# Cross attention with scores over row halves of the tensor engine, and a written-out round for every engine

## What is computed

```python
x = _layernorm(x + _L0_attn_ref(x, ...))                 # causal self-attention, 16 heads of 8
x = _layernorm(x + _L0_xattn_ref(ctx_1024, x, mask, ...))
x = _layernorm(x + _L0_ffn_ref(x, ...))                  # 8 experts, top 2, and a shared one

def _L0_xattn_ref(x, latents, mask, g1, b1, g2, b2, Wq, Wkv, Wout):
    heads, dim_head = (16, 64)
    xn = layer_norm(x, g1, b1)                           # 512 context rows
    ln_lat = layer_norm(latents, g2, b2)                 # 256 tokens
    q = ln_lat @ Wq
    kv = jnp.concatenate([xn, ln_lat], axis=1) @ Wkv     # 768 keys
    ...
    weight = jnp.einsum('bhld,bhnd->bhln', q * scale, k * scale)
    weight = jax.nn.softmax(jnp.where(full_mask, weight, neg), axis=-1)
    out = jnp.einsum('bhln,bhnd->bhld', weight, v)
    return out @ Wout
```

## Time and profile before

| | us |
|---|---|
| median of 3 runs | 1220.61 |
| lowest, highest | 1219.43, 1220.95 |
| span of the profiled execution | 1221.5 |
| PE busy in it | 1123.2 (92%) |
| DVE busy | 879.1 (72%) |
| ACT busy | 755.0 (62%) |
| POOL busy | 418.3 (34%) |

### The profile page before, as it was taken

One profiled execution on the slowest core, in us unless ns is written; L12 is line 12 of the kernel. 1 busy time (PEld: TensorE's weight loads), 2 busy tenths in 40 slices (PEclk: granted clock), 3 DMA queues, 4 the chain that ended last, 5 costly groups with the idle time before them and its releaser, 6 DMA issues. The chain is left out here.

```text
span 1221.5 us, 29151 instructions
## 1 busy us (share of the span) xinstructions
PE 1123.2 (92%) x8775; PEld 967.0 (79%) x8775; DVE 879.1 (72%) x2777; ACT 755.0 (62%) x1779; POOL 418.3 (34%) x453
## 2 busy tenths in 40 slices
PE   2998898399999999989999989999999986899996
PEld 2877777278888888878888878888888866899996
DVE  3998897687777787867787857787876755555555
ACT  2998997377666766756776756776766754222222
POOL 4554453134433434433433432533433424000000
PEclk9999999699999999999999999999999996899998
DMA  5000021000000000000000000000000000000001
GB/s 172 7 6 5 5 87 40 1 1 1 1 2 1 2 2 2 1 4 2 2 2 1 2 4 2 1 1 1 2 2 1 2 1 1 1 1 0 0 1 35
DMA packets 11403, 12.31 MB, mean 10 GB/s; under 512 B 1152, under 2 KB 9344, under 8 KB 11136
## 3 DMA queue, kind: packets, MB, share of 16 engines
q1 hardware_dynamic: 8032, 5.90, 1.7%
q10 hardware_dynamic: 3232, 4.73, 1.2%
HBM read 9.57 MB, written 1.05 MB: 9 GB/s over the span
## 5 line engine op out<-in xcount | busy, mean ns | idle before, releaser
L803 POOL TENSOR_TENSOR xk_parts<-k_raw,xk_parts 64x768 fp32r<-64x768 f32 x128 | 236.5, 1848 | 444.2 <-DVE xk_parts L895 444.2
L919 DVE CUSTOM_DVE_ANT_0 xmasked<-ps,bar 128x768 f32<-128x768 f32 x256 | 244.2, 954 | 6.0 <-issue 1.6
L852 ACT ACTIVATE xprobs<-xmasked,xlow 128x768 f32<-128x768 f32 x256 | 238.1, 930 | 6.1 <-issue 5.3
L999 PE MATMUL ps<-xk_parts,xq_parts 128*128 128x512 f32 (+1 forms) x1024 | 232.9, 349 | 4.5 <-DVE xq_parts L900 2.7
L1005 PE MATMUL ps<-ident,xprobs 128*128 128x128 f32 x1536 | 215.0, 276 | 1.5 <-DVE xprobs_t L924 1.1
L999 PEld LDWEIGHTS ps<-xk_parts,xq_parts 128*128 128x128 f32 x1024 | 175.1, 190 | 28.9 <-DVE xq_parts L900 3.2
L1016 PE MATMUL ps<-xprobs_t,xvals 128*64 128x256 f32 x1536 | 179.9, 383 | 1.1 <-ACT xprobs_t L858 1.1
L1005 PEld LDWEIGHTS ps<-ident,xprobs 128*128 128x128 f32 x1536 | 169.3, 140 | 9.4 <-DVE xprobs_t L924 1.3
L1016 PEld LDWEIGHTS ps<-xprobs_t,xvals 128*64 128x64 f32 x1536 | 104.7, 137 | 57.9 <-issue 10.5
L924 DVE COPY xprobs_t<-ps 128x768 f32<-128x768 f32 x128 | 121.6, 950 | 4.5 <-PE ps L1005 4.5
L112 DVE MEMSET xspare<- 128x1 f32 x256 | 15.1, 59 | 148.5 <-PE ps L999 114.6
(11 more groups left out here) (183 smaller groups left out, 2395.4 us busy)
## 6 DMA issues: line engine op xcount, KB each, us to landing
w_up<-in_L_ffn_w SPq DMA_DIRECT2D x2, 1024.0 KB, 6.8
raw_kv<-in_L_xattn_Wkv ACTq DMA_DIRECT2D x1, 1024.0 KB, 5.3
x_in<-in_x SPq DMA_DIRECT2D x8, 128.0 KB, 2.2
out<-state SPq DMA_DIRECT2D x4, 256.0 KB, 2.6
raw_q<-in_L_xattn_Wq ACTq DMA_DIRECT2D x1, 512.0 KB, 6.6
keep_all<-in_mask_BxS_bk ACTq DMA_DIRECT2D x1, 512.0 KB, 14.0
wout<-in_L_xattn_Wout ACTq DMA_DIRECT2D x1, 512.0 KB, 6.7
w_up<-in_L_ffn_sw SPq DMA_DIRECT2D x2, 128.0 KB, 4.0
```

Of the source, the lines that this page charges most:

```text
L803: pool.tensor_tensor(k_parts[dst, i // 2 % 2, h, :], k_raw[src, :], k_parts[src, i // 2 % 2, h, :].bitcast(F32), ALU.subtract).then_inc(k_ ...
L852: nc.scalar.activation(probs[:, i % 4, :], masked[:, i % 4, :], ACT.Exp, scale=-1.0, bias=low[:, i % 4:i % 4 + 1], accum_out=sums[:, pair ...
L919: dve.tensor_tensor_reduce(masked[:, i % 4, :], slot(slots.place("S", i), KEYS), bar[:, par, :], 1.0, 3e38, ALU.add, ALU.min, low[:, i % 4 ...
L999: last = nc.tensor.matmul(slot(s, hi - lo, lo), q_parts[:, pair % 2, h, part, t * P:(t + 1) * P], k_parts[:, pair % 2, h, lo:hi], start=pa ...
```

## The change

The split parts are no longer stacked. `q_parts[:, i % 2, 0]` is the rounded q of both heads of a pair, `[..., 1]` its rest, each with head 0 on rows 0 to 63 and head 1 on rows 64 to 127; `k_parts` likewise. S1 makes the scores of both heads for one half of the queries: three products (high by high, high by rest, rest by high) of 64 rows each per head, head 0 and head 1 in turn, into two slots, which S0 and S1 take. Rest by rest is left out. TWICE is gone; HI, Q and LO are one instruction of 128 partitions per pair.

PSUM: three wide slots remain. Q, R, TX and OUT share one narrow bank (`NARROW_BANK`); PV has one bank (`HEADS_BANK`) in place of two. The order is written out: a round per pair for each engine, with the once-a-batch steps at fixed rounds.

```diff
-    pe_order = Order(B, UNITS, {
-        "S": (UNITS, -2.25), "K": (PAIRS, -5.75), "Q": (PAIRS, -7.25), "V": (PAIRS, -4),
...
+    def pe_round(p):
+        yield from (("S0", 2 * p), ("S1", 2 * p), ("PT", 4 * p - 2), ("Q", p + 1), ("K", p + 1), ("PT", 4 * p - 1),
+                    ("V", p + 1))
+        if p == 4:
+            yield "TC", 1
+        yield from (("S0", 2 * p + 1), ("S1", 2 * p + 1), ("PT", 4 * p), ("PV", p - 1), ("PT", 4 * p + 1), ("R", p - 1))
+        if p == 1:
+            yield "OUT", -1
+        if p == 3:
+            yield "TX", 1
+
+    def dve_round(p):
+        if p == 2:
+            yield from (("OUT", -1), ("NORMED", 1), ("BAR", 1))
+        if p == 5:
+            yield "Y", 1
+        yield from (("S", 4 * p), ("S", 4 * p + 1), ("PT", 2 * p - 1), ("RECIP", p - 1), ("NORM", p - 2),
+                    ("Q", p + 1), ("HI", p + 1))
+        yield from (("S", 4 * p + 2), ("S", 4 * p + 3), ("PT", 2 * p))
+
+    def act_round(p):
+        yield "R", p - 2
+        if p == 4:
+            yield "TX", 1
+        yield from (("PT", 2 * p - 1), ("Q", p + 1), ("EXP", 4 * p), ("K", p + 1), ("EXP", 4 * p + 1), ("V", p + 1))
+        if p == 4:
+            yield "TC", 1
+        yield from (("PT", 2 * p), ("EXP", 4 * p + 2), ("EXP", 4 * p + 3))
+
+    def pool_round(p):
+        if p == 5:
+            yield "Y", 1
+        yield from (("WIDE", p - 1), ("LO", p + 1))
...
+    NARROW = ("Q", "R", "TX", "OUT")
+    wide = Turns(pe_order, [k for k in full if k not in NARROW], SLOTS)
+    narrow = Turns(pe_order, NARROW, 1)
+    NARROW_BANK, HEADS_BANK = O_BANK, O_BANK + 1
...
+                if kind == "S1":
+                    pair, t = i // 2, i % 2
+                    pe.wait_ge(k_ready, b * PAIRS + pair + 1)
+                    pe.wait_ge(q_ready, b * PAIRS + pair + 1)
+                    places = wide.place("S0", i), s
                     for lo, hi in ((0, C), (C, KEYS)):
-                        for part in range(2):
-                            last = nc.tensor.matmul(slot(s, hi - lo, lo), q_parts[:, pair % 2, h, part, t * P:(t + 1) * P],
-                                                    k_parts[:, pair % 2, h, lo:hi], start=part == 0, stop=part == 1)
-                    last.then_inc(full["S"], 1)
+                        for n, (qp, kp) in enumerate(((0, 0), (0, 1), (1, 0))):
+                            for h in range(2):
+                                rows = slice(h * XD, (h + 1) * XD)
+                                last = nc.tensor.matmul(slot(places[h], hi - lo, lo),
+                                                        q_parts[rows, pair % 2, qp, t * P:(t + 1) * P],
+                                                        k_parts[rows, pair % 2, kp, lo:hi], start=n == 0, stop=n == 2)
+                    last.then_inc(full["S1"], 1)
...
-                    wait(pe, heads_ready, n - 1)
+                    wait(pe, heads_ready, n)
```

More of the change, by code:

```diff
@@ L21 @@
 from contextlib import ExitStack
+from functools import partial
 import concourse.bass as bass
@@ L79, in run, with __init__ @@
         one(self.batches, self.batches)
+class Sequence(Order):
+    def __init__(self, batches, rounds, counts, pattern):
+        self.batches = batches
+        self.steps = []
+        for p in range(rounds):
+            for kind, n in pattern(p):
+                rel, i = divmod(n, counts[kind])
+                self.steps.append((kind, rel, i))
+        for kind, count in counts.items():
+            assert sorted(i for k, _, i in self.steps if k == kind) == list(range(count)), kind
+        assert all(-1 <= rel <= 1 for _, rel, _ in self.steps)
 class Turns:
@@ L735, in cross_attention @@
     normed_ready = sem("x_normed_ready")
-    full = {k: sem(f"x_{k}_full") for k in ("TC", "TX", "K", "Q", "V", "S", "PT", "R", "OUT")}
+    full = {k: sem(f"x_{k}_full") for k in ("TC", "TX", "K", "Q", "V", "S0", "S1", "PT", "R", "OUT")}
     yc_ready, yx_ready = sem("x_yc_ready"), sem("x_yx_ready")
@@ L740, in cross_attention @@
     kh_done, k_ready = sem("x_kh_done"), sem("x_k_ready")
[L741 to L742 removed]
+    qh_done, q_ready = sem("x_qh_done"), sem("x_q_ready")
     v_ready = sem("x_v_ready")
@@ new lines, in pool_round @@
+    def pool_round(p):
+        if p == 5:
+            yield "Y", 1
+        yield from (("WIDE", p - 1), ("LO", p + 1))
+    once = {"OUT": 1, "TC": 1, "TX": 1}
+    pairs = {"K": PAIRS, "Q": PAIRS, "V": PAIRS, "R": PAIRS}
+    pe_order = Sequence(B, PAIRS, {**once, **pairs, "S0": XH, "S1": XH, "PT": UNITS, "PV": PAIRS}, pe_round)
+    dve_order = Sequence(B, PAIRS, {"S": UNITS, "PT": XH, "Q": PAIRS, "HI": PAIRS, "RECIP": PAIRS, "NORM": PAIRS,
+                                    "OUT": 1, "NORMED": 1, "BAR": 1, "Y": 1}, dve_round)
@@ L830, in emit @@
                     act.wait_ge(full["K"], b * PAIRS + i + 1)
-                    wait(act, k_ready, b * XH + 2 * i)
-                    nc.scalar.activation(k_raw[:, :], slot(slots.place("K", i), KEYS), ACT.Copy).then_inc(k_out, 1)
+                    wait(act, k_ready, b * PAIRS + i)
+                    nc.scalar.activation(k_raw[:, :], slot(wide.place("K", i), KEYS), ACT.Copy).then_inc(k_out, 1)
                 if kind == "Q":
                     act.wait_ge(full["Q"], b * PAIRS + i + 1)
[L835 to L839, removed]
+                    wait(act, full["S1"], b * XH + 2 * (i - 1))
+                    nc.scalar.activation(q_parts[:, i % 2, 0, :], narrow_bank(S),
+                                         ACT.Copy, scale=Q_SCALE).then_inc(qh_done, 1)
                 if kind == "V":
@@ L956, in emit @@
                 if kind in full:
-                    s = slots.place(kind, i)
-                    earlier = slots.before(kind, b, i)
+                    turns = narrow if kind in NARROW else wide
+                    s = turns.place(kind, i)
+                    earlier = turns.before(kind, b, i)
                     if earlier:
@@ L963, in emit @@
                     for n, j in enumerate(range(CT) if kind == "TC" else range(CT, KT)):
-                        last = nc.tensor.transpose(slot(s, P, n * P), normed[:, j, :], ident[:, :])
+                        last = nc.tensor.transpose((narrow_bank if kind == "TX" else partial(slot, s))(P, n * P), normed[:, j, :], ident[:, :])
                     last.then_inc(full[kind], 1)
```

102 lines of the change are left out of this document (38 added, 64 removed).

## The result

| | us |
|---|---|
| before, median | 1220.12 |
| after, median of 4 | 1265.11 (1263.31 to 1266.53) |
| after / before | 1.0366, 95% interval 1.0351 to 1.0381 |

The change makes the kernel 45 us slower. The forecast had it 20 slower: the sign is right, the size less than half. 1265 is above the range of the likeliest case (1224 to 1257), and inside only the wide one, 1208 to 1281. The profiled execution of after took 1263.31 us.

The account below looks back on a forecast made before the run. The prediction took the order and length of tensor work as the bound: -8.5 us from ordinary rounds and +28.2 from batch turns gave +19.7, so 1240 us. The likeliest case ranged from 1224 to 1257, 8 in 10 from 1208 to 1281.

Parts of the forecast that it names:

- Part 3: Ordinary round with the ring of three wide PSUM places: 11.09 us against 11.22, 8.5 us gained over 64 rounds.
- the walk: Step-by-step timing of one tensor-engine round, S1 first at 0, from group lengths and waits: 11.09 us.
- Part 4: Turn of a batch: added waits cost 4.03 us each, +28.2 us for seven turns.
- part (b): Batch turn: OUT, stats, NORMED and BAR in one vector-engine piece before the first mask make K wait 2.16 us more.
- part (a): Batch turn: OUT and TX each wait for the scalar engine to copy R from the shared bank, 0.64 us each.
- Part (c): Batch turn: with TC behind V, the second S1 waits for V's place, 0.49 us.
- part (d): Batch turn: Y ahead of a mask, 0.2 us.
- Part 1: Scores: row halves run in pairs, an S1 takes 1.30 us with its shape changes, 0.24 us gained a pair.
- halves in turn: Rival on the scores: row halves don't overlap, each S1 1.05 us longer, 134 us more, 1374 us; chance 9%.
- serial weight loads: Rival on the scores: products pair up but their weight loads don't, 38 us more, 1278 us; chance 12%.
- free change of shape: Rival on the scores: entering a row-halved shape costs nothing, 32 us less, 1208 us; chance 19%.
- Part 2: Vector engine and gpsimd lose cast, HI, Q and LO work that was off the path: worth nothing directly.

Follow-up runs that it names:

- full rows: S1 as two 128-row products per head in place of three 64-row ones: 1278.14 us in the changed kernel, 1227.62 us with the order moves and swap added.
- all moves: Changed kernel with R and OUT behind the first S1, K before Q in OUT's round, TC, NORMED and BAR moved, the mask's waits swapped: 1223.63 us.
- the first experiment: Changed kernel with S1 as two products over all 128 rows per head, in the new order and layout: 1278.14 us, ratio 1.0471 to the kernel before.

## Why the prediction was wrong in size

**Part 3, the ordinary round: this step failed.** It forecast 11.09 us, 0.13 less than before; measured 11.43, 0.21 more. Over the stage that is -8.5 (0.13 x 64 is 8.3) against +13.2, 22 of the 25 us that the forecast is short of. Some rows of the kernel before, from the pair of the earlier trace rows, that the walk did not use:

```profile
490.49 0.94 PE L999 MATMUL ps<-xk_parts,xq_parts 128*128 128x512 f32 x4
491.26 0.84 PE L1005 MATMUL ps<-ident,xprobs 128*128 128x128 f32 x6
491.96 0.39 PE L989 MATMUL ps<-wv_hi,y_hi 128*128 128x256 f32 x1
...
493.12 0.86 PE L999 MATMUL ps<-xk_parts,xq_parts 128*128 128x512 f32 x4
493.82 0.28 PE L978 MATMUL ps<-y_hi,wq_hi 128*128 128x256 f32 x1
```

The round by its groups, each from its start to the start of the next, any wait behind it included:

| us | before | walk | after |
|---|---|---|---|
| scores (four groups, now two) | 2.98 | 2.60 | 2.51 |
| four PT | 2.65 | 2.60 | 2.72 |
| R | 0.19 | 0.22 | 0.31 |
| PV | 2.74 | 2.84 | 2.74 |
| Q | 0.37 | 0.56 | 0.66 |
| K | 1.13 | 1.05 | 1.15 |
| V | 1.16 | 1.22 | 1.34 |
| round | 11.22 | 11.09 | 11.43 |

The first four lines of the walk are off by little in sum (0.02): PT and R are longer than it had them, the scores and PV shorter. Q, K and V are 0.32 of the 0.34 that the round is short of. K waits 0.30 behind Q and not 0.20; its products take 1.15 and not 1.05; V with the wait for the vector engine's copy of PT takes 1.34 and not 1.22.

Two mistakes stand behind that. First, the walk built its groups from the spacing of single products and set their sum against a measured round. The same pieces add up to 10.98 for the kernel before, 0.24 less than its 11.22, and K at 1.13 and V at 1.16 stand in its rows. Pieces against pieces, the walk says 0.11 more than before and not 0.13 less. By my estimate that is 7 us more over 64 rounds, and a forecast of 1256 in place of 1240. Second, the waits were sized too small. Moving R into the gap ahead of K took 0.21 off the round, and the swap of the mask's two waits 0.16, which shows that K's wait for the mask is on the path. The wait of 0.18 between V and S1 is the same with full rows (1.34), so it is not due to row halves; no run took it away.

**Part 4, the turns: right in mechanism and nearly in size.** Forecast 4.03 us for a turn and 28.2 for seven. Measured: (17.92 - 11.43) + (13.36 - 11.43) - 4.33 = 4.09 for a turn of the one kind, 0.4 less for the other, and 26.6 for all with the stage's start and end. Moving NORMED and BAR away shows part (b), and moving OUT shows part (a). Part (c), S1 waiting for V's place, is there with 0.52 (V to TC and TC to S1 are 1.15 and 1.15, less TC's 0.44 and an ordinary 1.34); part (d), 0.2 for Y, is not: Q to K is 0.67 in that round. The clock fell in two turns, 3 us and not 13.

**Part 1, the pairing of row halves: right.** The rivals of halves in turn (1374) and of serial weight loads (1278) fall by S1's 1.27 us; the second would have had 1.60. The rival of a free change of shape falls too: in the pair of kernels that differ in the shape alone, what stands beside two S1 groups is 0.29 longer. The Trainium skill, TensorEngine Tiling (Array Packing), section Key Properties, says that changing the tiling mode drains the engine; by that rule the trace agrees, with this 0.29. The Trainium skill lets tiles load and multiply in parallel in the same section (TensorEngine Tiling (Array Packing), Key Properties), and the 256-column pairs bear that out with 0.12 from pair to pair. An S1 with its edges is 1.25 + 0.15 = 1.40 against the forecast 1.30, and against full rows in the same order a pair of heads gains 0.17; the walk had 0.24.

**Not forecast: the jump of the outer loop.** 2.6 us for two jumps beyond before. The idle time is put down to issue. With the row-halved products a jump costs 5 us more in after and 4.6 in all moves, by a longer idle stretch and by the clock behind it. It isn't the number of instructions alone, for the kernel before has as many score products as the full rows, and its jump costs 5.8 where theirs costs 2.0 to 2.1. What it depends on stays open; it wasn't tried.

The 58 us that order and layout lose together can't be told apart by the first experiment. Moves in the order and the swap alone, on the same layout and full rows, return 50 of them. That leaves 8 us for the layout and what the order still costs.

**Part 2:** 250 us less work on the other engines brought nothing that shows. No run tested it by itself.

## What to carry to other kernels

Before you free time on engines that aren't the bound, walk the bound engine's order with its ring of buffers, and walk the kernel before with the same pieces first. Here the pieces fell 0.24 us short of its measured round, more than the whole gain that the walk then forecast (0.13). Use the measured distance from group to group where a row has it. Once-a-batch work put in one piece ahead of what the bound engine waits for (here 3.3 to 3.7 us ahead of a mask) cost 1.8 to 2.2 us each time; put it behind what others wait for. Where two waits stand ahead of a latency-critical instruction, put the one that ends last at the end, and measure it: it gave 9 us here on one engine, nothing in the kernel before, and on the tensor engine the same idea lost 3.

## What the runs showed of the hardware

- The order in which products for two row halves are issued doesn't matter: with three of one head and then three of the other, a group of twelve still takes 1.26 us (one run), where one after the other would be 2.1.
- Going into row halves and out costs 0.29 us for two groups of scores with their neighbours, where the products themselves gain 0.46.
- The first product of 512 columns behind a wait is 0.33 us from the second, behind transposes 0.31, and 0.23 in a stream: part of the weight load of 128 columns shows.
- An idle stretch at a loop's jump is 4.94 us long in one kernel and 1.57 in another of the same order. Behind the long one the granted clock was at the lower level for 6.8 us, behind the short one not at all.
